# Gated residual on one core: each chunk's 128 partitions split between two DMA queues

## The reference, cut to what matters

```python
def reference(x, cond_1024, W1, b1, W2, b2):          # x: 128 x 128 x 512 f32; cond: 128 x 512
    h = jax.nn.silu(cond_1024 @ W1.T + b1)
    gate = jax.nn.sigmoid(h @ W2.T + b2)[:, None, :]  # 128 x 1 x 512
    # the Haar transform of x along its middle axis, every coefficient times gate,
    # and the inverse transform: it gives x * gate, since gate doesn't vary along that axis
    return x + (x + x * gate)
```

## Time and profile before

| | us |
|---|---|
| median of 3 runs (lowest to highest) | 166.78 (166.63 to 167.11) |
| the profiled execution | 166.82 |
| its span, first to last instruction | 165.1 |
| what lies outside the span (the difference) | 1.7 |
| VectorE busy | 80.0 |
| TensorE busy | 22.7 |
| mean rate of the DMA queues over the span | 421 GB/s |

### The profile page before, as it was taken

The page is one execution under the profiler, slowest core; times in us unless marked ns, Lnnn a source line. Parts: engine busy times, 40 slices in busy tenths (PEclk is TensorE's granted clock), DMA queues, the critical chain, the costliest instruction groups (busy, mean ns, idle before and its releaser), DMA issues.

```text
span 165.1 us, 219 instructions
## 1 busy us (share of the span) xinstructions
PE 22.7 (14%) x68; PEld 12.2 (7%) x68; DVE 80.0 (48%) x20; ACT 2.5 (2%) x3; POOL 2.6 (2%) x10
## 2 busy tenths in 40 slices
PE   0099969800000000000000000000000000000000
PEld 0093722300000000000000000000000000000000
DVE  0052380499999999999970000000004999700000
ACT  3000100100000000000000000000000000000000
POOL 6000000000000000000000000000000000000000
PEclk9999987995555555555555555555555555555555
DMA  5999969969998997989997996999899799799995
GB/s 151 474 456 508 476 286 508 508 286 476 508 397 365 508 508 254 508 349 413 508 429 334 508 508 302 461 508 413 349 508 445 334 492 508 318 445 405 445 421 254
DMA packets 1732, 69.47 MB, mean 421 GB/s; under 512 B 194, under 2 KB 194, under 8 KB 324
## 3 DMA queue, kind: packets, MB, share of 16 engines
q1 hardware_dynamic: 1008, 43.25, 61.4%
q10 hardware_dynamic: 724, 26.22, 36.9%
HBM read 35.92 MB, written 33.55 MB: 421 GB/s over the span
## 4 chain that ended last, share of the span: by engine, by line
DMA 50%; DVE 19%; PE 12%; DVEq 5%; ACT 1%; issue 0%
DMA ring<-in_x 23%; DMA out<-ring 22%; DVE ring L242 10%; DVE ring L247 5%; DVEq L30 5%; DMA ring<-in_L_cond_W 5%; PE gate_sum L173 3%; PE turned L181 2%; PE hidden_sum L151 2%; PE turned L135 2%; DVE ring L229 2%; PE hidden_sum L146 1%; PE turned_cond L140 1%; DVE factor L237 0%; DVE ring L222 0%; ACT ring L193 0%
## 5 line engine op out<-in xcount | busy, mean ns | idle before, releaser
L242 DVE TENSOR_TENSOR ring<-ring,factor 128x16384 f32<-128x16384 f32 x3 | 51.5, 17220 | 0.0
L247 DVE TENSOR_TENSOR ring<-ring,factor 128x8192 f32<-128x8192 f32 x2 | 17.3, 8688 | 40.5 <-DMA ring<-in_x 40.5
L216 DVE COPY ring<-turned 128x512 f32<-128x512 f32 x4 | 2.8, 692 | 10.0 <-PE turned L135 10.0
L237 DVE TENSOR_SCALAR factor<-turned 128x512 f32<-128x512 f32 x4 | 2.8, 691 | 6.9 <-PE turned L181 6.9
L173 PE MATMUL gate_sum<-ring 128*128 128x512 f32 x8 | 5.4, 833 | 1.3 <-DVE ring L227 1.3
L135 PE MATMUL turned<-identity,ring 128*128 128x128 f32 x16 | 3.6, 423 | 8.4 <-DMA ring<-in_L_cond_W 8.4
L229 DVE COPY ring<-turned 128x512 f32<-128x512 f32 x4 | 3.9, 1056 | 0.0
L135 PEld LDWEIGHTS turned<-identity,ring 128*128 128x128 f32 x16 | 3.3, 227 | 8.4 <-issue 8.4
L181 PE MATMUL turned<-ring 128*128 128x512 f32 x8 | 3.7, 601 | 0.8 <-ACT ring L193 0.8
L151 PE MATMUL hidden_sum<-ring 128*128 128x512 f32 x8 | 3.7, 605 | 0.0
L222 DVE TENSOR_TENSOR ring<-hidden_sum,ring 128x512 f32<-128x512 f32 x1 | 0.7, 692 | 5.6 <-ACT ring L190 5.6
(11 more groups left out here) (17 smaller groups left out, 6.6 us busy)
## 6 DMA issues: line engine op xcount, KB each, us to landing
out<-ring ACTq DMA_DIRECT2D x2, 4096.0 KB, 20.8
ring<-in_L_cond_W ACTq DMA_DIRECT2D x1, 1024.0 KB, 7.7
ring<-in_L_cond_W SPq DMA_DIRECT2D x1, 1024.0 KB, 7.5
ring<-in_cond SPq DMA_DIRECT2D x1, 256.0 KB, 7.7
ring<-in_x SPq DMA_DIRECT2D x3, 34.6
b_row<-in_L_cond_b ACTq DMA_DIRECT2D x2, 2.0 KB
out<-ring SPq DMA_DIRECT2D x2, 45.6
ring<-in_x ACTq DMA_DIRECT2D x1, 38.6
```

The costliest lines, as they stand in the source:

```text
L216: dve.tensor_copy(w1_t[:, c, :], turned[c][:, :]).then_inc(w1_t_set, 1)
L242: dve.tensor_tensor(ring[:, c, :, :], ring[:, c, :, :], steps_of(c, STEPS), ALU.mult).then_inc(chunk_scaled, 1)
L247: dve.tensor_tensor(ring[:, 0, piece(h), :], ring[:, 0, piece(h), :], steps_of(CHUNKS - 1, PIECE), ALU.mult).then_inc(chunk_scaled, 1)
```

## The change

Every transfer of a chunk of `x` or `out` is now two transfers. Partitions 0 to 63 go through SP's queue and partitions 64 to 127 through ACT's. Both queues carry the same list: load chunks 0 and 1; after the last gate product, load chunk 2; store chunk 0; store the first 16 steps of chunk 1; once this queue's own half of chunk 0 is stored, load chunk 3; store the other 16 steps of chunk 1; store chunk 2; store chunk 3 in two halves. VectorE waits for both halves of a chunk (32 completions in place of 16); its instructions are the same. `W1` and `cond` remain on SP's queue, and `W2`, `b1` and `b2` on ACT's. Bytes, and the size of the piece that one partition gets in one transfer (64 KB; 32 KB where 16 steps are moved), are as before, but chunk 1's store is now in two pieces of 16 steps.

```diff
+        SP_PARTS, ACT_PARTS = slice(0, P // 2), slice(P // 2, P)
+        BOTH = 2 * DMA_DONE
...
         def _(sp):
             sp.dma_start(w1_rows, w1.rearrange("(p t) k -> p t k", t=BLOCKS)).then_inc(w1_loaded, DMA_DONE)
             sp.dma_start(cond_rows, cond).then_inc(cond_loaded, DMA_DONE)
             for c in range(SCRATCH):
-                sp.dma_start(ring[:, c, :, :], chunk(x_parts, c)).then_inc(chunk_loaded[c], DMA_DONE)
+                sp.dma_start(ring[SP_PARTS, c, :, :], chunk(x_parts, c)[SP_PARTS]).then_inc(chunk_loaded[c], DMA_DONE)
             sp.wait_ge(gate_spread, GROUPS)
-            sp.dma_start(ring[:, SCRATCH, :, :], chunk(x_parts, SCRATCH)).then_inc(chunk_loaded[SCRATCH], DMA_DONE)
-            for c in range(SLOTS - 1):
-                sp.wait_ge(chunk_scaled, c + 1)
-                sp.dma_start(chunk(out_parts, c), ring[:, c, :, :]).then_inc(chunk_stored[c], DMA_DONE)
+            sp.dma_start(ring[SP_PARTS, SCRATCH, :, :],
+                         chunk(x_parts, SCRATCH)[SP_PARTS]).then_inc(chunk_loaded[SCRATCH], DMA_DONE)
+            sp.wait_ge(chunk_scaled, 1)
+            sp.dma_start(chunk(out_parts, 0)[SP_PARTS], ring[SP_PARTS, 0, :, :]).then_inc(sp_stored0, DMA_DONE)
+            sp.wait_ge(chunk_scaled, 2)
+            sp.dma_start(chunk(out_parts, 1)[SP_PARTS, piece(0), :],
+                         ring[SP_PARTS, 1, piece(0), :]).then_inc(sp_stored1, DMA_DONE)
+            sp.wait_ge(sp_stored0, DMA_DONE)
+            sp.dma_start(ring[SP_PARTS, 0, :, :],
+                         chunk(x_parts, SLOTS)[SP_PARTS]).then_inc(chunk_loaded[SLOTS], DMA_DONE)
+            sp.dma_start(chunk(out_parts, 1)[SP_PARTS, piece(1), :],
+                         ring[SP_PARTS, 1, piece(1), :]).then_inc(sp_stored1, DMA_DONE)
+            sp.wait_ge(chunk_scaled, SLOTS)
+            sp.dma_start(chunk(out_parts, SLOTS - 1)[SP_PARTS],
+                         ring[SP_PARTS, SLOTS - 1, :, :]).then_inc(sp_stored2, DMA_DONE)
+            for h in range(PIECES):
+                sp.wait_ge(chunk_scaled, CHUNKS + h)
+                sp.dma_start(chunk(out_parts, CHUNKS - 1)[SP_PARTS, piece(h), :],
+                             ring[SP_PARTS, 0, piece(h), :]).then_inc(sp_stored3, DMA_DONE)
...
         def _(act):
...
             act.dma_start(b2_row[:, :], b2.rearrange("(a j) -> a j", a=1)).then_inc(b2_loaded, DMA_DONE)
+            for c in range(SCRATCH):
+                act.dma_start(ring[ACT_PARTS, c, :, :], chunk(x_parts, c)[ACT_PARTS]).then_inc(chunk_loaded[c], DMA_DONE)
...
-            act.wait_ge(chunk_stored[0], DMA_DONE)
-            act.dma_start(ring[:, 0, :, :], chunk(x_parts, SLOTS)).then_inc(chunk_loaded[SLOTS], DMA_DONE)
+            act.wait_ge(gate_spread, GROUPS)
+            act.dma_start(ring[ACT_PARTS, SCRATCH, :, :],
+                         chunk(x_parts, SCRATCH)[ACT_PARTS]).then_inc(chunk_loaded[SCRATCH], DMA_DONE)
...
             for c in range(CHUNKS - 1):
-                dve.wait_ge(chunk_loaded[c], DMA_DONE)
+                dve.wait_ge(chunk_loaded[c], BOTH)
```

More of the change, by code:

```diff
@@ L13 @@
 SLOTS = 3
-LAST_PIECES = 2
+PIECES = 2
 DMA_DONE = 16
@@ L21, in gated_residual_program @@
     CHUNKS = N // STEPS
-    PIECE = STEPS // LAST_PIECES
+    PIECE = STEPS // PIECES
     PER_GROUP = CHUNKS // GROUPS
@@ L79, in gated_residual_program @@
         chunk_scaled = sem("chunk_scaled")
-        chunk_stored = [sem(f"chunk_stored{c}") for c in range(CHUNKS)]
-        last_stored = [sem(f"last_stored{h}") for h in range(1, LAST_PIECES)]
+        sp_stored0, sp_stored1, sp_stored2, sp_stored3 = [sem(f"sp_stored{c}") for c in range(CHUNKS)]
+        act_stored0, act_stored1, act_stored2, act_stored3 = [sem(f"act_stored{c}") for c in range(CHUNKS)]
         block = ctx.enter_context(nc.Block())
@@ L99, in _ @@
             for c in range(SCRATCH):
-                sp.dma_start(ring[:, c, :, :], chunk(x_parts, c)).then_inc(chunk_loaded[c], DMA_DONE)
+                sp.dma_start(ring[SP_PARTS, c, :, :], chunk(x_parts, c)[SP_PARTS]).then_inc(chunk_loaded[c], DMA_DONE)
             sp.wait_ge(gate_spread, GROUPS)
-            sp.dma_start(ring[:, SCRATCH, :, :], chunk(x_parts, SCRATCH)).then_inc(chunk_loaded[SCRATCH], DMA_DONE)
-            for c in range(SLOTS - 1):
-                sp.wait_ge(chunk_scaled, c + 1)
-                sp.dma_start(chunk(out_parts, c), ring[:, c, :, :]).then_inc(chunk_stored[c], DMA_DONE)
+            sp.dma_start(ring[SP_PARTS, SCRATCH, :, :],
[17 more added lines that the diff above has]
+                             ring[SP_PARTS, 0, piece(h), :]).then_inc(sp_stored3, DMA_DONE)
+            sp.wait_ge(sp_stored1, PIECES * DMA_DONE)
+            sp.wait_ge(sp_stored2, DMA_DONE)
+            sp.wait_ge(sp_stored3, PIECES * DMA_DONE)
         @block.gpsimd
@@ L193, in _ @@
             act.activation(gate, gate_sum[:, :], ACT.Sigmoid).then_inc(gate_set, 1)
-            act.wait_ge(chunk_stored[0], DMA_DONE)
-            act.dma_start(ring[:, 0, :, :], chunk(x_parts, SLOTS)).then_inc(chunk_loaded[SLOTS], DMA_DONE)
+            act.wait_ge(gate_spread, GROUPS)
+            act.dma_start(ring[ACT_PARTS, SCRATCH, :, :],
+                         chunk(x_parts, SCRATCH)[ACT_PARTS]).then_inc(chunk_loaded[SCRATCH], DMA_DONE)
+            act.wait_ge(chunk_scaled, 1)
+            act.dma_start(chunk(out_parts, 0)[ACT_PARTS], ring[ACT_PARTS, 0, :, :]).then_inc(act_stored0, DMA_DONE)
@@ new lines, in _ @@
+            act.wait_ge(chunk_scaled, 2)
+            act.dma_start(chunk(out_parts, 1)[ACT_PARTS, piece(0), :],
+                         ring[ACT_PARTS, 1, piece(0), :]).then_inc(act_stored1, DMA_DONE)
+            act.wait_ge(act_stored0, DMA_DONE)
+            act.dma_start(ring[ACT_PARTS, 0, :, :],
+                         chunk(x_parts, SLOTS)[ACT_PARTS]).then_inc(chunk_loaded[SLOTS], DMA_DONE)
+            act.dma_start(chunk(out_parts, 1)[ACT_PARTS, piece(1), :],
+                         ring[ACT_PARTS, 1, piece(1), :]).then_inc(act_stored1, DMA_DONE)
@@ L198, in _ @@
             act.wait_ge(chunk_scaled, SLOTS)
-            act.dma_start(chunk(out_parts, SLOTS - 1), ring[:, SLOTS - 1, :, :]).then_inc(chunk_stored[SLOTS - 1], DMA_DONE)
-            done = [chunk_stored[CHUNKS - 1]] + last_stored
-            for h in range(LAST_PIECES):
+            act.dma_start(chunk(out_parts, SLOTS - 1)[ACT_PARTS],
+                         ring[ACT_PARTS, SLOTS - 1, :, :]).then_inc(act_stored2, DMA_DONE)
+            for h in range(PIECES):
                 act.wait_ge(chunk_scaled, CHUNKS + h)
-                act.dma_start(chunk(out_parts, CHUNKS - 1)[:, piece(h), :],
-                              ring[:, 0, piece(h), :]).then_inc(done[h], DMA_DONE)
@@ L207, in _ @@
[L207 to L210, removed]
+                act.dma_start(chunk(out_parts, CHUNKS - 1)[ACT_PARTS, piece(h), :],
+                             ring[ACT_PARTS, 0, piece(h), :]).then_inc(act_stored3, DMA_DONE)
+            act.wait_ge(act_stored1, PIECES * DMA_DONE)
+            act.wait_ge(act_stored2, DMA_DONE)
+            act.wait_ge(act_stored3, PIECES * DMA_DONE)
@@ L240, in _ @@
             for c in range(CHUNKS - 1):
-                dve.wait_ge(chunk_loaded[c], DMA_DONE)
+                dve.wait_ge(chunk_loaded[c], BOTH)
                 dve.tensor_tensor(ring[:, c, :, :], ring[:, c, :, :], steps_of(c, STEPS),
                                   ALU.mult).then_inc(chunk_scaled, 1)
-            dve.wait_ge(chunk_loaded[CHUNKS - 1], DMA_DONE)
-            for h in range(LAST_PIECES):
+            dve.wait_ge(chunk_loaded[CHUNKS - 1], BOTH)
+            for h in range(PIECES):
                 dve.tensor_tensor(ring[:, 0, piece(h), :], ring[:, 0, piece(h), :], steps_of(CHUNKS - 1, PIECE),
```

## The result

The changed kernel takes 273.52 us (median of 4 runs, 273.02 to 273.60) against 166.70 for the kernel before: 1.640 times as long, 95% interval 1.638 to 1.642. The prediction's likeliest case said 169.2. The time lies in the range only because the range was drawn to take in the rivals. The case was the wrong one: what came is the rival "halves at half rate", at a lower price than that rival had.

A forecast was written before the change was run, and what follows sets the result against it. The prediction took the kernel as bound by bytes, DMA engines 98.3% busy and every wait covered. Only the late `cond` added time: 166.82 + 2.4 = 169.2 us, with an 8 in 10 range of 167.5 to 312.

The forecast's parts named there:

- likeliest case: Whole kernel: `cond` lands late, half-partition transfers keep full rate, engines idle 2.4 us; 169.2 us, chance 0.42.
- halves at half rate: Chunk transfers: engines in step all work on one partition half at a time, 217 GB/s; 300 to 320 us, chance 0.30.
- The bound, and how queues are served: DMA engines: bytes bound the kernel; each engine takes one packet per queue in turn, 2.42 us per 64 KB row.
- The rival by which `cond` is through in a turn or two: Load of `cond`: small packets aren't slowed, it lands by 13.8, the time stays 166.8 us; chance 0.12.
- The chain behind `cond`: Gate after `cond` lands at 25.9: 21.15 + 1.6 us, chunk 2's load issued at 48.7, engines dry for 2.4 us.
- Chunk 3's load in the middle of chunk 1's store: VectorE gets chunk 3 about 10 us earlier, its cover of 10 us becomes 20; no time gained.
- The step that failed: Transfers over 64 partitions: taken at the full 432 GB/s, so halves cost nothing; the other value was 217 GB/s.
- Half rate, engines apart: Chunk transfers: same limit, but engines alternate between halves and lose only where one queue works alone; 201 to 300 us, chance 0.12.

The follow-up runs named there:

- e2: Kernel after, but the two queues split each chunk by steps, each on all 128 partitions: 167.03 us, ratio 1.001.
- e5: Kernel before, with chunk 1 loaded whole by ACT's queue, so that `cond` takes turns with large rows: 174.63 us, ratio 1.046.
- e14: Kernel after, with SP's queue on the even partitions and ACT's on the odd ones in place of halves: 172.79 us, ratio 1.036.
- e6: Kernel after, but both queues wait until `cond` has landed before the first load of a chunk: ratio 1.539, runs of 255.1 to 264.3 us.
- e7: e6 with an 8-row HBM to HBM transfer added ahead of chunk 0 on SP's queue, meant to shift engines: 274.17 us, ratio 1.640.
- e10: e6 with 12 KB loaded into each of partitions 0 to 7 ahead of chunk 0 on SP's queue, to shift engines: 275.02 us, ratio 1.652.
- e1: No kernel: transfers of `x` and `out` alone, in stages over different partitions; loads of partitions 0 to 63 ran at 205 GB/s.
- e13: No kernel: loads alone, partitions and HBM rows changed apart; the same 32 rows ran at 189 GB/s into partitions 0 to 31, 308 into every fourth.
- e11: Kernel before, with its loads alone issued as partition halves on the same queue, stores whole: 249.62 us, ratio 1.495.
- e12: Kernel before, with its stores alone issued as partition halves on the same queue, loads whole: 229.17 us, ratio 1.371.
- e9: No kernel: transfers alone in stages, some engines held back by a 16 KB load to partitions 0 to 7; both halves' load rows took 4.95 us.
- e15: No kernel: loads alone in stages, some by 8 engines; partitions 0 to 63 ran at 204 GB/s with 8 engines, every other partition 2.42 us a row.
- e8: No kernel: transfers alone in stages, with an HBM to HBM transfer meant to hold engines back; rows of partitions 0 to 15 took 7 to 10 us.
- e4: Kernel after, with `cond` loaded ahead of `W1` on SP's queue: 262.71 us, ratio 1.569.

## Why the prediction was wrong

**The bound, and how queues are served: right.** The kernel is bound by bytes, and the engines stay at 98% busy. They take turns row by row: `cond` landed at 18.7 with rows of 32 KB beside it (e2), at 28.4 with eight rows of 64 KB (e5), and at 25.85 in e14, for which the prediction has 25.9. The rival by which `cond` is through in a turn or two is refuted for these transfers, and with it what the Trainium skill has of a turn, 9 to 17 descriptors ("DMA: Bandwidth & Descriptors", "Queues, rings and completion order").

**The chain behind `cond`: right in size.** In e14, where its assumption of full rate holds, the last gate product ended at 48.75 (prediction 48.7), the chain took 22.85 us (prediction 21.15 + 1.6), and the engines stood still from 47.4 to 50.0: 2.6 us for the 2.4 predicted. The first rows after the pause took about 3.1 us each, 0.7 more than usual. The profiled execution of e14 is 171.25, so 4.4 us above that of before: 3.3 are these two. Of the other 1.1, the start and length of the packets in the trace place about 0.6 just before 47.4, where the engines ran dry one after another, and 0.4 at the very end. Why the median is another 1.5 us higher I did not find. The term was also put into the wrong frame: in the kernel after, with rows of 5.07 us, `cond` came at 46.1 (42.8 by the half-rate rival). What that costs there stays open: with `cond` in time e6 took 17 us less, but e7 and e10 took as long as the kernel after.

**Chunk 3's load in the middle of chunk 1's store: right, and worth nothing.** VectorE got chunk 3 at 116.7 in e2, 9 us earlier than before for the 10 predicted, and the time stayed the same.

**The step that failed** is "I take the first value for the sum, as the nearest row has it": a transfer over 64 partitions at full rate. It was the one step without a row, and the nearest row was of the kind that could not tell, since every large transfer of the kernel before covers all partitions and so shows nothing of what fewer partitions get. The runs put a row of a half at 5.0 to 5.1 us for loads and for stores on one queue and at 4.95 for loads on two (e1), and show that the partitions covered decide it (e13, e14). It is worth 101 of the 107 us (273.5 against 172.8 for even and odd partitions).

The Trainium skill had this outright, and the runs agree with it: "SBUF — State Buffer", "Door 1: The DMA port swizzle", lets partitions 0 to 63 reach 8 of 16 ports of 27 GB/s, and 0 to 3 a single one; measured were 196 and 27 GB/s (e13). By its section "Can I just issue two DMAs to hit both halves?" two concurrent halves gained 6% over one; here the loads of e1 had rows of 4.93 us on the mean with both halves at once and 5.03 with one, 2%. I gave the rule a chance of 0.42 in two rivals and the full rate 0.42 in the sum.

**The rival's price was too high**, 300 to 320 for 273.5. The missing part is in the windows: 210 GB/s with loads on both queues, but 315 where ACT stores beside SP's loads and 312 from 200 us on. A store row of a half takes 2.6 us where it takes turns with load rows of 4.6 (e1), and stores on both queues get faster for a while, from 5.2 us to 3.3 and less. Of the 153 us by which the rival's 320 lies above the kernel before, 46 did not come, and by these rows I put them down to the kernel's mixed stretches and its stores; no run sizes that share. e11 and e12 size the two kinds in the kernel before at 83 and 62 us.

**"Half rate, engines apart"** had 273.5 within its 201 to 300, but by luck. It assumed that engines on opposite halves relieve each other fully. They don't: load rows stay at 4.95 to 5.1 us with 3, 6 or 8 of 16 engines on the other half (e10, e9, e15). So being in step, which the first rival gave as the reason, isn't the cause either. What two engines on opposite halves share stays open; that 8 engines suffice for a half's whole rate is the nearest that was measured.

## What to carry to other kernels

Before a transfer is cut by partitions, ask which groups of partitions its pieces reach: cut by steps or by even and odd partitions, or leave it whole. If a price has no row in the trace, the nearest row is no evidence when it was taken under the one condition that the change removes; a documented rule then weighs more. And keep small transfers on which a chain hangs out of a queue whose neighbour holds large rows: each of their packets waits for one row.

## What was not expected of the hardware

- A whole chunk loaded beside a whole chunk stored, on two queues, ran at 328 GB/s in e1 (rows of 2.4 to 4.5 us), where the kernel before has 437 in a like stretch (15.73 MB in 36 us). The same stage in e8 ran at 330 GB/s. Not followed up.
- Loads of halves by two queues keep 4.95 us a row to the end; stores of halves drift, from 5.2 us to 3.3 on the mean some 15 us later, with single rows of 2.4, and then up again to 5.1 in some.
- A transfer of 8 rows from HBM to HBM was spread over all 16 engines (16 packets of 32 KB), one of 8 partitions into the memory over 8.
- With large rows in the other queue, moving `cond` ahead of `W1` only hands the delay on: `W1` landed at 40.1 (e4).
